# A two-layer decoder on one core: the softmax chain in a new order, and squares summed as bf16 pairs

## What is computed

```python
def rmsnorm(x, g, eps=EPS):
    var = jnp.mean(jnp.square(x), axis=-1, keepdims=True)
    return x * jax.lax.rsqrt(var + eps) * g
q, k = rmsnorm(x @ Wq, gq), rmsnorm(ctx @ Wk, gk)      # per head, layer 0's cross attention
scores = jnp.einsum('bqhd,bkhd->bhqk', q, k) * scale   # causal mask in both self attentions
attn = jax.nn.softmax(scores, axis=-1)
out = jnp.einsum('bhqk,bkhd->bqhd', attn, v)           # then @ Wo, residual, LayerNorm
```

## Time and profile before

| what | value |
|---|---|
| median of 3 runs | 2929.32 us (2920.0 to 3839.74) |
| the profiled execution's own time | 2923.55 us |
| its span, first to last instruction | 2921.7 us |
| mean granted TensorE clock | 0.945 of full speed (2.4 GHz) |
| PE, DVE, ACT, POOL busy | 86%, 64%, 54%, 30% of the span |

### The profile page before, as it was taken

How to read it: one execution, slowest core, us unless ns; L and a number is a source line. 1 busy time by engine, 2 the same in 40 slices (tenths; PEclk the granted TensorE clock), 3 DMA queues, 4 the chain that set the end, 5 groups by cost and what they waited for, 6 DMA issues and landing times. The chain is left out here.

```text
span 2921.7 us, 60581 instructions
## 1 busy us (share of the span) xinstructions
PE 2509.2 (86%) x21768; PEld 1612.3 (55%) x21768; DVE 1862.7 (64%) x3317; ACT 1572.5 (54%) x2742; POOL 864.7 (30%) x741
## 2 busy tenths in 40 slices
PE   6888888888888898888978999989999999986454
PEld 4555555455655565566455666655566666643222
DVE  4666663366665666666155666651688888858886
ACT  4666663176766666666043555550577777732321
POOL 4556555400110010012232212223100000146675
PEclk9999998999999999999988999999999999998777
DMA  3333333144444444446230333341477777852000
GB/s 96 71 71 92 68 73 81 47 89 92 97 95 91 95 91 96 93 94 124 80 151 21 85 88 87 88 94 46 84 146 145 143 151 145 153 115 77 20 0 29
DMA packets 752867, 263.39 MB, mean 90 GB/s; under 512 B 724816, under 2 KB 724816, under 8 KB 751184
## 3 DMA queue, kind: packets, MB, share of 16 engines
q1 hardware_dynamic: 750960, 255.48, 41.0%
q0 software_dynamic: 1760, 5.77, 0.7%
HBM read 82.84 MB, written 2.10 MB: 29 GB/s over the span
## 5 line engine op out<-in xcount | busy, mean ns | idle before, releaser
L786 ACT ACTIVATE ph<-p,ri 128x1024 bf16<-128x1024 f32 (+4 forms) x512 | 437.4, 854 | 461.6 <-DVE ri L1056 394.9
L1066 DVE SCALAR_TENSOR_TENSOR pl<-p,ri,ph 128x1024 bf16<-128x1024 f32 (+4 forms) x512 | 517.4, 1010 | 129.6 <-issue 83.5
L1122 PE MATMUL ps<-wo_hi,v_hi 128*128 128x128 bf16 x2688 | 487.2, 222 | 79.4 <-DMA wo_lo<-pl 79.3
L1123 PE MATMUL ps<-wo_lo,v_hi 128*128 128x128 bf16 x2688 | 487.0, 222 | 0.0
L1124 PE MATMUL ps<-wo_hi,v_lo 128*128 128x128 bf16 x2688 | 486.9, 222 | 0.0
L797 ACT ACTIVATE p<-p,nb 128x1024 f32<-128x1024 f32 (+4 forms) x512 | 435.7, 851 | 48.4 <-DVE nb L1049 33.9
L1122 PEld LDWEIGHTS ps<-wo_hi,v_hi 128*128 128x128 bf16 x2688 | 266.7, 99 | 142.9 <-DMA wo_lo<-pl 96.0
L1122 PE MATMUL ps<-k_hi,q_hi 128*128 128x512 bf16 (+3 forms) x768 | 277.2, 361 | 45.9 <-issue 30.1
L1123 PEld LDWEIGHTS ps<-wo_lo,v_hi 128*128 128x128 bf16 x2688 | 266.9, 99 | 39.1 <-issue 0.8
L1124 PE MATMUL ps<-k_hi,q_lo 128*128 128x512 bf16 (+3 forms) x768 | 277.1, 361 | 0.0
L1123 PE MATMUL ps<-k_lo,q_hi 128*128 128x512 bf16 (+3 forms) x768 | 276.9, 361 | 0.0
(11 more groups left out here) (197 smaller groups left out, 6066.4 us busy)
## 6 DMA issues: line engine op xcount, KB each, us to landing
raw_kv<-in_wkvself SPq DMA_DIRECT2D x32, 512.0 KB, 3.9
raw_q<-in_wqself SPq DMA_DIRECT2D x32, 256.0 KB, 2.7
wo_hi<-ph SPq DMA_TRANSPOSE x512, 3.1
wo_lo<-pl SPq DMA_TRANSPOSE x512, 3.1
raw_q<-in_woself SPq DMA_DIRECT2D x32, 256.0 KB, 2.8
raw_q<-in_wqcross SPq DMA_DIRECT2D x32, 256.0 KB, 2.7
raw_q<-in_wocross SPq DMA_DIRECT2D x32, 256.0 KB, 3.0
raw_kv<-in_wkvcross SPq DMA_DIRECT2D x24, 256.0 KB, 3.1
```

Of the source, the lines that this page charges most:

```text
L786: nc.scalar.activation(m["ph"][:, qt % 2, 0:w], m["p"][:, qt % 2, 0:w], ACT.Copy, scale=ri[:, qt % 2:qt % 2 + 1]).then_inc(p_norm, 1)
L1066: nc.vector.scalar_tensor_tensor(out=m["pl"][:, qt % 2, 0:w], in0=m["p"][:, qt % 2, 0:w], scalar=ri[:, qt % 2:qt % 2 + 1], in1=m["ph"][:, ...
L1122: nc.tensor.matmul(o, l(0), r(0), start=first, stop=False)
L1123: nc.tensor.matmul(o, l(0), r(1), start=False, stop=False)
```

## The change

Five things change.
- ACT does `rounded` for the current step right behind its exp, and not for the step before ahead of it. DVE does `inverse` for the current step behind `remainder` of the step before. `heads_out` goes behind `job_parts` on both engines. DVE's `remainder` stays one step behind.
- In cross0 ACT does `key_norms` in step 3 ahead of the exp, behind the wait for the maxima, and not at the end of step 2.
- The semaphore of the transposes is split in two: `rounded` waits for that of ph alone, `remainder` for that of pl, PE for both.
- In cross0 the square sq is split by POOL into a bf16 pair, and the sums of squares are two bf16 matmuls in place of one float32 matmul.
- In cross0 KN0 goes behind K1, and KN1 behind Q.

```diff
         if self.rms:
-            plan = [[("K", 0)], [("KN", 0), ("K", 1)], [("KN", 1), ("Q", 0)], [("QN", 0), ("V", 0), ("V", 1)]]
+            plan = [[("K", 0)], [("K", 1), ("KN", 0)], [("Q", 0), ("KN", 1)], [("QN", 0), ("V", 0), ("V", 1)]]
...
-                    sp.dma_start_transpose(m["pT"][0][:, qt, 0:w // P, :], m["ph"][:, qt % 2, 0:w]).then_inc(tr_in[qt], 16)
+                    sp.dma_start_transpose(m["pT"][0][:, qt, 0:w // P, :], m["ph"][:, qt % 2, 0:w]).then_inc(tr_hi[qt], 16)
...
-                    sp.dma_start_transpose(m["pT"][1][:, qt, 0:w // P, :], m["pl"][:, qt % 2, 0:w]).then_inc(tr_in[qt], 16)
+                    sp.dma_start_transpose(m["pT"][1][:, qt, 0:w // P, :], m["pl"][:, qt % 2, 0:w]).then_inc(tr_lo[qt], 16)
...
+                def split_squares(n, it, qt, jobs):
+
+                    for kind, half in jobs:
+                        if kind not in ("K", "Q"):
+                            continue
+                        s = 2 if kind == "Q" else half
+                        count = lambda n: c["sq"] + 3 * (n + 1) + s + 1
+                        pool.wait_ge(sq_ok, at(count, n, it))
+                        if n >= 0 or s:
+                            pool.wait_ge(job_mm, at(lambda n: c["job"] + squares_free(n, s), n, it))
+                        pool.nop(nofuse=True)
+                        nc.gpsimd.tensor_scalar(m["sqs"][0][:, :], m["sq"][:, :], 1.0, 1.0, ALU.mult, ALU.mult).then_inc(sq_hi, 1)
+                        pool.wait_ge(sq_hi, at(count, n, it))
+                        pool.nop(nofuse=True)
+                        nc.gpsimd.tensor_tensor(m["sqs"][1][:, :], m["sq"][:, :], m["sqs"][0][:, :], ALU.subtract).then_inc(sq_lo, 1)
+
+                def squares_free(n, s):
+
+                    return L.before(n - 1, 3) + 1 if s == 0 else L.before(n, 1) + 2 if s == 1 else L.before(n, 2) + 2
...
                             if L.rms:
+                                s = 2 if kind == "Q" else half
+                                act.wait_ge(sq_lo, at(lambda n: c["sq"] + 3 * (n + 1) + s, n, it))
                                 nc.scalar.activation(m["sq"][:, :], bank, ACT.Square).then_inc(sq_ok, 1)
...
                     for qt in range(QT):
-                        if n or qt:
-                            rounded(*((n, it, qt - 1) if qt else (n - 1, it, QT - 1)))
                         act.wait_ge(s_max, at(lambda n: CREDIT + c["s"] + QT * n + qt + 1, n, it))
                         prob = m["p"][:, qt % 2, 0:L.width(qt)]
+                        if L.rms and qt == QT - 1:
+                            key_norms(n, it, qt - 1, L.jobs(n, qt - 1))
...
                         nc.scalar.activation(prob, prob, ACT.Exp, scale=1.0 if L.rms else -1.0, bias=nb[:, qt % 2:qt % 2 + 1], accum_out=rs[:, qt % 2:qt % 2 + 1]).then_inc(p_exp, 1)
+                        rounded(n, it, qt)
+                        job_parts(n, it, qt, L.jobs(n, qt))
                         if qt == QT - 1 and n:
                             heads_out(n - 1, it)
-                        job_parts(n, it, qt, L.jobs(n, qt))
                         if L.rope and qt > 0:
                             rotated(n, it, qt - 1, L.jobs(n, qt - 1))
-                        if L.rms:
-                            key_norms(n, it, qt, L.jobs(n, qt))
...
                     for qt in range(QT):
                         prior = (n, it, qt - 1) if qt else (n - 1, it, QT - 1)
-                        if n or qt:
-                            inverse(*prior)
                         scores(n, it, qt)
                         if n or qt:
                             remainder(*prior)
+                        inverse(n, it, qt)
+                        job_parts(n, it, qt, L.jobs(n, qt))
                         if qt == QT - 1 and n:
                             heads_out(n - 1, it)
-                        job_parts(n, it, qt, L.jobs(n, qt))
...
-                        pe.wait_ge(sq_ok, at(lambda n: c["sq"] + 3 * (n + 1) + half + 1, n, it))
-                        last = nc.tensor.matmul(bank, ones[:, :], m["sq"][:, :], start=True, stop=True)
+                        pe.wait_ge(sq_lo, at(lambda n: c["sq"] + 3 * (n + 1) + half + 1, n, it))
+                        nc.tensor.matmul(bank, onesb[:, :], m["sqs"][0][:, :], start=True, stop=False)
+                        last = nc.tensor.matmul(bank, onesb[:, :], m["sqs"][1][:, :], start=False, stop=True)
```

More of the change, by code:

```diff
@@ L137, in build @@
         ones = sb("ones", [P, P], F32)
+        onesb = sb("onesb", [P, P], BF16)
         idx = sb("idx", [P, IT], I32)
@@ L152, in build @@
         job_mm, job_hi, job_lo = sem("job_mm"), sem("job_hi"), sem("job_lo")
-        sq_ok, k_log, k_norm, q_norm = sem("sq_ok"), sem("k_log"), sem("k_norm"), sem("q_norm")
+        sq_ok, sq_hi, sq_lo, k_log, k_norm, q_norm = sem("sq_ok"), sem("sq_hi"), sem("sq_lo"), sem("k_log"), sem("k_norm"), sem("q_norm")
         rope_sum, rope_hi, rope_lo = sem("rope_sum"), sem("rope_hi"), sem("rope_lo")
@@ L156, in build @@
         p_lo, o_mm, o_hi, o_lo = sem("p_lo"), sem("o_mm"), sem("o_hi"), sem("o_lo")
-        tr_in = [sem(f"tr_in{i}") for i in range(QT)]
+        tr_hi, tr_lo = [sem(f"tr_hi{i}") for i in range(QT)], [sem(f"tr_lo{i}") for i in range(QT)]
         y_mm, y_add, ln_var, ln_rstd, ln_x = sem("y_mm"), sem("y_add"), sem("ln_var"), sem("ln_rstd"), sem("ln_x")
@@ L279, in build @@
                 m["sq"] = sb("sq", [P, S], F32, s)
+                m["sqs"] = [sb(f"sq_{k}", [P, S], BF16, s) for k in hl]
                 m["rk"] = sb("rk", [P, 2, SC], F32, s)
@@ L458, in _ @@
             nc.gpsimd.tensor_scalar(idb[:, :], ident[:, :], 1.0, 1.0, ALU.mult, ALU.mult).then_inc(idb_ok, 1)
+            nc.gpsimd.tensor_scalar(onesb[:, :], ones[:, :], 1.0, 1.0, ALU.mult, ALU.mult).then_inc(idb_ok, 1)
             def split_hi(hi, src):
@@ L603, in unit @@
                         if L.rms:
+                            split_squares(n, it, qt, L.jobs(n, qt))
                             query_norms(n, it, qt, L.jobs(n, qt))
@@ L619, in _ @@
                     if L.rms:
+                        split_squares(-1, None, qt, L.jobs(-1, qt))
                         query_norms(-1, None, qt, L.jobs(-1, qt))
@@ L783, in rounded @@
                     if bn >= 0:
-                        act.wait_ge(tr_in[bq], at(lambda n: 32 * (c["u"] + behind(n, qt, 2)[0] + 1), n, it))
+                        act.wait_ge(tr_hi[bq], at(lambda n: 16 * (c["u"] + behind(n, qt, 2)[0] + 1), n, it))
                     act.wait_ge(r_inv, at(lambda n: c["s"] + QT * n + qt + 1, n, it))
@@ L816, in _ @@
                 units(act, unit)
-                rounded(UNITS - 1, None, QT - 1)
                 heads_out(UNITS - 1, None)
@@ L1062, in remainder @@
                     if bn >= 0:
-                        dve.wait_ge(tr_in[bq], at(lambda n: 32 * (c["u"] + behind(n, qt, 2)[0] + 1), n, it))
+                        dve.wait_ge(tr_lo[bq], at(lambda n: 16 * (c["u"] + behind(n, qt, 2)[0] + 1), n, it))
                     dve.wait_ge(p_norm, at(lambda n: c["s"] + QT * n + qt + 1, n, it))
@@ L1096, in _ @@
                 units(dve, unit)
-                inverse(UNITS - 1, None, QT - 1)
                 remainder(UNITS - 1, None, QT - 1)
@@ L1259, in job @@
                     elif kind == "KN":
-                        pe.wait_ge(sq_ok, at(lambda n: c["sq"] + 3 * (n + 1) + half + 1, n, it))
-                        last = nc.tensor.matmul(bank, ones[:, :], m["sq"][:, :], start=True, stop=True)
+                        pe.wait_ge(sq_lo, at(lambda n: c["sq"] + 3 * (n + 1) + half + 1, n, it))
+                        nc.tensor.matmul(bank, onesb[:, :], m["sqs"][0][:, :], start=True, stop=False)
+                        last = nc.tensor.matmul(bank, onesb[:, :], m["sqs"][1][:, :], start=False, stop=True)
                     elif kind == "QN":
-                        pe.wait_ge(sq_ok, at(lambda n: c["sq"] + 3 * (n + 1) + 3, n, it))
+                        pe.wait_ge(sq_lo, at(lambda n: c["sq"] + 3 * (n + 1) + 3, n, it))
                         for q in range(QT):
-                            last = nc.tensor.matmul(bank[:, q:q + 1], m["sq"][:, q * P:q * P + P], ones[:, 0:1], start=True, stop=True)
+                            nc.tensor.matmul(bank[:, q:q + 1], m["sqs"][0][:, q * P:q * P + P], onesb[:, 0:1], start=True, stop=False)
+                            last = nc.tensor.matmul(bank[:, q:q + 1], m["sqs"][1][:, q * P:q * P + P], onesb[:, 0:1], start=False, stop=True)
                     last.then_inc(job_mm, 1)
@@ L1272, in weigh @@
                         pe.wait_ge(o_lo, at(lambda n: CREDIT + c["u"] + n - 1, n, it))
-                    pe.wait_ge(tr_in[qt], at(lambda n: 32 * (c["u"] + n + 1), n, it))
+                    pe.wait_ge(tr_hi[qt], at(lambda n: 16 * (c["u"] + n + 1), n, it))
+                    pe.wait_ge(tr_lo[qt], at(lambda n: 16 * (c["u"] + n + 1), n, it))
                     v, blocks = L.kvslot(n), L.width(qt) // P
```

(2 more changed lines are left out.)

## The result

| kernel | median | ratio to the kernel before | span of the profiled execution |
|---|---|---|---|
| before | 2927.48 us (4 runs) | 1 | 2921.7 us |
| after | 3257.66 us (3253.99 to 3262.58, 4 runs) | 1.1138, 95% interval [1.1115, 1.1161] | 3252.1 us |

The change makes the kernel 11.4% slower. The forecast was 3308, in a range of 3120 to 3450. The ratio leaves out one run of the kernel before, of 3839.74 us.

A forecast was written before the change was run, and what follows sets the result against it. PE was taken as the nominal bound, but the DVE-ACT chain as the bound in cross0's job steps. Terms 198 + 105 + 74 + 8 = +385 over the profiled 2923.55 gave 3308 us, range 3120 to 3450.

The forecast's parts named there:

- The chain: In a step with a job, the new softmax order puts every link in one line: +1.45 us at width 1024.
- cross0, forecast +198: In cross0, steps add +5.4 us a unit and the clock +1: 31 x 6.4 = +198 us (130 to 260).
- The term of +1 for the clock: In cross0, V1 and weigh behind PE's idle gap run partly at 1.2 GHz: +1 us a unit, between 0 and 2.6.
- The pairs and the plan: In cross0, evacuating KN0 and KN1 costs 0.67 us each in steps 1 and 2; POOL's split costs nothing.
- self0, forecast +74: In self0, ph's length and hand-overs add +2.4 us a unit over 31 units: +74 us (40 to 95).
- the shared port: In cross0, pl beside a POOL instruction would lengthen the chain; costed at nothing, 65 us as the high end.
- cross1, forecast +105: In cross1, a PE-bound pair of 31.5 us becomes 38.3: +6.8 times 15.5 = +105 us (60 to 115).
- self1, forecast +8: In self1, up to +2.4 us a unit, but PE hides most: +8 us (-15 to +74).
- What the profile was to show: Cross0's step 0 at 6.1 us, V1 5.2 behind scores, ph's idle time under 0.2, pl-transpose waits near nothing.
- the faster one: Rival: PE stays last in every step, so float32 passes and transposes' waits count: 2814 us, chance 0.06.
- the one of no effect: Rival: the jobs' hi half today waits for PE, not exp, so ph fits in the gap: 2925 us, chance 0.04.
- the half absorbed: Rival: shorter hand-overs and idle stretches filled by moved work absorb half: about +200, 3125 us, chance 0.14.

The follow-up runs named there:

- Experiment 3: The changed kernel with ACT doing the jobs' hi halves ahead of ph: 3005.3 us, ratio 1.0274.
- experiment 4: The changed kernel with key_norms back at the end of step 2: 3181.0 us, ratio 1.0875.
- experiments 1: The changed kernel with float32 squares, the old plan and key_norms at the end of step 2: 3116.4 us, ratio 1.0657.
- experiments 2: The kernel before with the bf16 pairs and the new plan alone: 3018.6 us, ratio 1.0326.
- experiment 8: The changed kernel with ph last in ACT's step, key_norms back, nq evacuated ahead of the reciprocal, float32 sums and the old plan: 2806.9 us, ratio 0.961.
- experiment 6: The changed kernel with POOL's split of self0's projection weights cut to one column: 3226.6 us, ratio 1.1047.
- experiments 7: The changed kernel with ph last in ACT's step, key_norms back, nq evacuated ahead of the reciprocal, bf16 pairs kept: 2808.2 us, ratio 0.9611.
- experiment 9: Semaphore split added to the kernel before (2875.3 us), added with heads_out behind job_parts (2834.1 us), and undone in the ph-last float32 kernel (2843.5 us).

## Why the prediction was right, and where its terms were off

**The chain** was right, link for link, in steps 0 to 2 and in V1's start. Step 0 of cross0 takes 5.94 to 6.00 us (6.1 forecast), V1 starts 5.26 behind the scores (5.2), a job step of cross1 takes 5.00 to 5.07 (5.3) and a step without one 2.77 (2.77), self0's even units 15.9 (13.44 + 2.4 = 15.8). Experiment 3 is the proof: ph off the path, 252 us less.

The total owes something to luck: the sum was 55 us above the growth of 330, and of that 41 are the missing term below, while self0 came 26 over its term and cross1 and self1 25 under theirs.

**cross0, forecast +198, measured +146.** A term was left out. Against the kernel with the split semaphore alone, cross0 grew from 746.8 to 934.5, +188, and a unit from 23.89 to 29.86, +5.97, for the 6.4 forecast (steps +1.35, +1.94, +0.59, +2.1, where I had +1.45, +2.1, +0.9, and 0.95 with 1 for the clock). The split gave 41 back. The forecast gave the split no place in cross0 and took the kernel before as one length per unit; a look at the four units of a pass one by one would have shown that every fourth step 3 took 12.92 in the mean where its neighbours took 8.67 to 9.51, and that the cause stood under "issue". What PE's instruction fetch did could not have been foretold from the rows, but that these 41 us hung on something other than the chain could.

The Trainium skill, "Runtime: NRT & Kernel Launch", section "Instruction fetch mechanics", says that PE holds 128 KiB of instructions, 2048, refilled in blocks of 16 KiB. It says too that a taken branch whose target is not in the current window of two blocks forces a fetch before execution goes on. The trace agrees in the packets' size (1.00 MB in 61, 16.4 KB each) and in the stall's place, the turn of the loop. It does not agree with a window of two blocks: cross1's loop of 648 matmuls and as many weight loads, and cross0's of 816 after the change, turn back without a packet, and the measurement decides. From the earlier trace rows, cross0's pass over 4 units has 816 matmuls (5305/26 x 4) and as many weight loads, self0's and self1's some 458 and cross1's 648, so the longest loop alone has it. Which boundary the loop must not cross was not tried; only that a shift of 33 instructions is enough.

**The key norms' place**, two passes of 1.06 and a slower clock, was part of the same step 3, and experiment 4 prices it at 77 us, 2.5 a unit. The term of +1 for the clock stands in size: from V1 to the next scores took 1.6 us more in 18 of 24 units, 1.2 in the mean, behind 3.06 us of idle time (3.6 forecast). In the kernel with the split alone, behind 2.30 us, it was 2 of 24. Its two parts were not as I had them: V1 kept 1.35 us, and `weigh` took 2.73 in place of 1.3.

**The pairs and the plan** I cost at 0.67 in each of steps 1 and 2 and POOL's part at nothing. With the old order around the key norms they cost 63 us in cross0 (experiments 1 and 4), 2.0 a unit, of which 0.6 are in step 1 and about 0.7 each in steps 2 and 3. KN0's sum starts 2.0 us late (61.6/31), double what I gave it, and is covered, as said. In step 3 QN's sum starts 1.5 late and is covered as well, with the key norms in either place: in experiments 2 and 4 it stands ready some 3 to 5 us before nq is taken out. What costs in step 3 there is the plan: KN1's evacuation behind q_lo lets the key norms start later, and exp and nq with them. So no wait for POOL shows on the path, as forecast (no run takes POOL's part out alone), and the plan has a price in step 3 that the forecast did not give it. How much of that the change itself pays, with the key norms behind the maxima anyway, no run separates. The price of PE's float32 passes was never paid on the path: experiment 8 has them and is not slower.

**self0, forecast +74, measured +100.** The chain's +2.4 a unit was right in even units; the odd ones grew by 4.3. The mis-sized term is the shared port, which I weighed for cross0 alone, as the high end. Here it took 30 us (experiment 6). The kernel before has these meetings too, with less effect: k_lo takes 1.02 us in its odd units (2.35 after the change) for 0.69 in even ones, and its odd units are 0.4 us longer, not 2.4. (In the sum of this term 4 x 0.3 is 1.2, not 1.1; that is 3 us in the stage.) The Trainium skill, "SBUF — State Buffer", section "SBUF: two separate sides", has VectorE with two SBUF inputs wait for a whole GpSimd instruction that started first; by that rule, too, k_lo at 304.12 ends only behind wkv_lo (305.89), and the trace agrees: 306.44 less 305.89 is 0.55, a little less than its own 0.69. The pl beside it starts 0.03 us ahead of POOL's subtraction and is long all the same, which the rule does not give; but spans on POOL are rough.

**cross1, forecast +105, measured +87.** The links are 5% shorter than those from cross0's rows (5.0 for 5.3: 0.20 for 0.26 to ph, 1.05 for 1.13 behind it, 0.61 each for 0.70 and 0.67), so a pair takes 37.4 in place of 38.3; PE is 88% busy, and not 83%. **self1, forecast +8, measured +0.8:** PE hides it.

**What the profile was to show** came in the step lengths. PE's wait for pl's transposes did not vanish, it is 65.1 us for 79.3, 28.8 of it in self1, which is PE's stage still, and 13.7 in cross1, for 4.0 before. ph's idle time is 0.29, not under 0.2, and ph holds 1% of the chain that ended last.

The rivals: the faster one is excluded by PE's falling share, the one of no effect as well. That of the half absorbed had a wrong mechanism: what absorbed 41 us was no idle stretch filled by moved work, but a stall that went.

## What to carry to other kernels

An instruction of one engine that needs an answer from another (ph needs the reciprocal, the reciprocal exp's sums) goes last in its step, where it fills the wait for the next step's input; ahead of work that someone waits for, it costs its own length and two hand-overs in each step. In an unrolled loop compare the passes' units one by one, and the step at the turn above all: a step that is long once a pass, under "issue", with many packets in the instruction queue, points to fetched instructions, and 33 idle instructions ahead of the loop cured it here. Measure parts of a change against a kernel that has the same instruction placement, or else that effect (1.0 to 1.8% here) is put down to the part.

The fastest kernels of this study are those of experiments 7 and 8, 3.9% under the one before. By the pairs of experiment 9, 1.0 to 1.8 points of such a gain come from the place of the loop, the rest from the order.

## What the runs showed of the hardware

- Instructions of a long loop on PE are fetched again in every pass, or in none behind the first, by where the loop lies: 114 or 60 to 61 packets of 16.4 KB. PE then stalls for 3.3 to 3.9 us at each turn and goes on at 1.2 GHz: 41 us over six turns, 6.9 each.
- Behind an idle stretch of 3.06 us the way from V1 to the next scores took 6.0 to 6.2 us in place of 4.4 in 18 of 24 units, with PE at 1.2 GHz (in the unit shown from 1.4 us behind V1's start on). Behind one of 2.30 us it did in 2 of 24 (the split alone) and in 5 of the 19 units away from the turn (the kernel before), and behind 1.8 us or less (experiments 1, 4, 7, 8) in none. The mean over the window also holds other waits: it is 0.98 in experiment 4 and 0.99 with the split alone.
- A VectorE instruction with two SBUF operands beside a POOL subtraction of 1024 columns took 2.32 us for 0.69, a bf16 remainder beside one of 512 columns 1.60 for 0.61.
- The hand-over from DVE to ACT (reciprocal to ph) was 0.26 us from start to start in cross0 and 0.20 in a step of cross1 with a job.
